# Batch 1's second pair summed on the vector engine, the tail put in another order, and empty slots that carry row numbers

## The reference

```python
xn = layernorm(x)                                   # x: [8, 512, 128]
# s: attention of each token over its own 16 heads (no sum over tokens)
q = xn @ Wq + bq                                    # [8, 512, 16, 8]
k, v = split((xn @ Wdown + bdown) @ Wup + bup)      # the same shape each
att = softmax(einsum('bthd,btgd->bthg', rope(q), rope(k)) / sqrt(8))
s = einsum('bthg,btgd->bthd', att, v) @ Wout + bout
# g: a transformer block on xn; its sequence is the batch axis (8, causal),
# then a mixture of 8 experts, 2 for each token, at most 1280 rows each
h1 = xn + proj(causal_attention(ln1(xn)))
z = ln2(h1)
p, i = top_k(softmax(z @ router), 2)                # p divided by its sum
h = h1 + sum over a token's 2 experts of p * gelu(z @ w1[i]) @ w2[i]
return x + s * silu(h)
```

## Time and profile before

| | us |
|---|---|
| median of 3 executions | 464.91 |
| lowest, highest | 464.27, 466.33 |
| the profiled execution | 464.99 |
| its span | 463.2 |
| mean granted PE clock (share of full speed) | 0.849 |

### The profile page before, as it was taken

The page is one execution under the profiler, slowest core; times in us unless marked ns, Lnnn a source line. Parts: engine busy times, 40 slices in busy tenths (PEclk is TensorE's granted clock), DMA queues, the critical chain, the costliest instruction groups (busy, mean ns, idle before and its releaser), DMA issues.

```text
span 463.2 us, 4715 instructions
## 1 busy us (share of the span) xinstructions
PE 337.6 (73%) x1518; PEld 247.7 (53%) x1518; DVE 382.1 (82%) x505; ACT 172.8 (37%) x382; POOL 254.4 (55%) x282
## 2 busy tenths in 40 slices
PE   1678986847834758864839997966999569739992
PEld 1565664635723623762626975745777356514852
DVE  5999599967979993799974986999997999780694
ACT  3475365262437100100104308626548544502311
POOL 0579446400005776877737757566977667537502
PEclk9955899786977659895869998988999797979997
DMA  8899910000000111011149112311234111149301
GB/s 206 151 193 200 316 49 2 0 0 2 0 0 29 53 52 52 2 52 52 52 124 257 51 35 59 114 60 53 80 110 121 57 40 47 40 140 297 91 0 45
DMA packets 53558, 38.06 MB, mean 82 GB/s; under 512 B 5337, under 2 KB 50206, under 8 KB 53534
## 3 DMA queue, kind: packets, MB, share of 16 engines
q1 hardware_dynamic: 48926, 28.25, 24.9%
q0 software_dynamic: 4608, 9.51, 6.1%
HBM read 16.55 MB, written 21.20 MB: 82 GB/s over the span
## 4 chain that ended last, share of the span: by engine, by line
PE 35%; DVE 18%; issue 17%; ACT 7%; another core or an unknown queue 3%; DMA 1%; SPq 0%; DVEq 0%; ACTq 0%
PE banks L944 10%; PE banks L916 5%; PE banks L923 4%; PE banks L931 4%; DVE prod L276 4%; PE banks L969 3%; DVE score L615 3%; PE banks L777 2%; ACT flat L1226 2%; DVE prod L285 1%; ACT flat L1240 1%; PE banks L955 1%; PE banks L957 1%; DVE stat L377 1%
## 5 line engine op out<-in xcount | busy, mean ns | idle before, releaser
L1326 POOL DMA_INDIRECT slot_rows<-rows_all,scatter_at x64 | 62.2, 972 | 75.9 <-DVE scatter_at L590 56.9
L1358 POOL DMA_INDIRECT expert_rows<-flat,to_at x80 | 79.1, 989 | 33.0 <-issue 21.5
L944 PE MATMUL banks<-prod,c_identf 128*128 128x256 f32 x256 | 62.8, 405 | 9.5 <-issue 9.2
L1301 POOL TENSOR_TENSOR prod<-rows_all,block_kv 128x64 f32<-128x64 f32 (+3 forms) x64 | 48.7, 796 | 36.9 <-ACT block_kv L1086 36.8
L944 PEld LDWEIGHTS banks<-prod,c_identf 128*128 128x128 f32 x256 | 52.4, 206 | 20.3 <-issue 12.1
L916 PE MATMUL banks<-flat 128*128 128x512 f32 (+1 forms) x96 | 41.0, 576 | 8.3 <-ACT flat L1226 6.4
L276 DVE TENSOR_TENSOR prod<-banks,qkv_h 128x2048 f32<-128x2048 f32 x20 | 44.8, 2282 | 0.6 <-DVE score L615 0.5
L615 DVE TENSOR_REDUCE score<-prod 128x512 f32<-128x4096 f32 x10 | 44.2, 4420 | 0.3
L285 DVE TENSOR_TENSOR prod<-score,banks 128x2048 f32<-128x2048 f32 x16 | 35.6, 2281 | 10.7 <-PE banks L931 10.5
L802 PE MATMUL banks<-wx,qkv_h 128*128 128x128 f32 x192 | 32.0, 328 | 11.9 <-ACT qkv_h L1105 6.7
L276 POOL TENSOR_TENSOR qkv_h<-block_kv,qkv_h 128x2048 f32<-128x2048 f32 x8 | 35.9, 4507 | 6.8 <-ACT block_kv L1110 6.7
(11 more groups left out here) (190 smaller groups left out, 586.0 us busy)
## 6 DMA issues: line engine op xcount, KB each, us to landing
slot_rows<-prod SPq DMA_DIRECT2D x10, 528.0 KB, 12.6
flat<-slot_rows SPq DMA_DIRECT2D x16, 264.0 KB
expert_rows<-prod SPq DMA_DIRECT2D x8, 512.0 KB, 6.9
flat<-expert_rows SPq DMA_DIRECT2D x8, 512.0 KB, 7.4
xn_all<-in_x SPq DMA_DIRECT2D x4, 512.0 KB, 4.9
flat<-in_w SPq DMA_DIRECT2D x16, 128.0 KB
out<-rows_all SPq DMA_DIRECT2D x7, 256.0 KB, 2.3
expert_rows<-flat,to_at POOLq DMA_INDIRECT x80
```

Source lines behind the costliest of these rows:

```text
L944: i = M.matmul(head_bank(s)[:, 2 * p * D:2 * (p + 1) * D].rearrange("p (a h d) -> p a h d", a=2, h=H), C["identf"][:], value_pair(s, p).re ...
L1301: Q.tensor_tensor(from_key(0, par, t).rearrange("p l (m d) -> p l m d", d=HD), q[:, :, t * QH:], block_key(h, par, t).unsqueeze(2).broadca ...
L1326: Q.indirect_dma_start(slots_d, bass.IndirectOffsetOnAxis(ap=scatter_at[:, k, n:n + 1], axis=0), z2x[:, h, s, part], None, element_offset= ...
L1358: Q.indirect_dma_start(expert_d, bass.IndirectOffsetOnAxis(ap=to_at[:, e % 2, a:a + 1], axis=0), ye[:, e % 2, a, :], None).then_inc(ye_out ...
```

## The change

**Empty slots.** The fill of the slots is no longer zeros. POOL clears a block of 128 x 2 x 10 x 132 floats (`empty`) at its start, waits for the constants and writes numbers of rows of `expert_rows` that nobody reads into column 1 (`TENSOR_SCALAR`, 20 elements for each partition). SP fills from it with 20 DMAs instead of 10, in a layout with 128 rows of each expert together. `expert_rows` is three rows longer. A slot of a second choice keeps the filled number in column 1, so DVE takes it off the number that it writes at the other end: two small steps more before `diff_done`, one more behind the slots' reduce, one less at the numbers.

**read_slots** keeps three of six operations (the steps that put numbers in the place of zeros are gone). Gates and numbers have three buffers instead of two, so that it waits for the work of e - 3, where it waited for e - 1 and e - 2; the scatters of e now wait for those of e - 2 themselves. The experts run in the order 0, 4, 1, 5, 2, 6, 3, 7 (`ORDER`).

The diff, cut to its core (`...` marks what is left out):

```diff
-PE_SCORES, SCORE_BANK = 1, (0, 7)
-
+PE_SCORES, SCORE_BANK = 1, 0
...
+
+AMID_SLOTS = {11: 0, 22: 1}
...
+ORDER = [i // 2 + i % 2 * (E // 2) for i in range(E)]
...
-EXPONENTIAL_AFTER = {0: 3, 2: 4, 7: 6}
+
+FIRST_EMPTY = 3
+
+EXPONENTIAL_AFTER = {0: 3, 2: 4}
...
-TAIL_BANKS = 4
-LAST_TURNED, LAST_OUT = (6, 0), (1, 2)
+TAIL_BANKS, PE_ROWS = 4, 6
+
+LAST_TURNED, LAST_OUT = (6, 0), (2, 3)
...
-    expert_d = nc.dram_tensor("expert_rows", (SLOTS + TOPK * CAP, D), F32, kind="Internal").ap()
+    expert_d = nc.dram_tensor("expert_rows", (SLOTS + TOPK * CAP + FIRST_EMPTY, D), F32, kind="Internal").ap()
...
-            sp.wait_ge(W["zero_done"], 1)
-            for k in range(CT):
-                sp.dma_start(slots_d[k * E * P:(k + 1) * E * P, :].rearrange("(p a) d -> p a d", p=P),
-                             zeros.broadcast_to([P, E, ROW])).then_inc(W["zero_out"], 16)
+            sp.wait_ge(W["empty_made"], 1)
+            for par in range(2):
+                for a in range(CT):
+                    sp.dma_start(slots_d[0:SLOTS, :].rearrange("(r e a p) d -> p r a e d", r=2, a=CT, p=P)[:, par, a],
+                                 empty[:, par, a:a + 1, :].broadcast_to([P, E // 2, ROW])).then_inc(W["zero_out"], 16)
...
                 sp.dma_start(expert_d[1 + s * E * P:1 + (s + 1) * E * P, :].rearrange("(p a) d -> p a d", p=P),
-                             zeros[:, :, 0:D].broadcast_to([P, E, D])).then_inc(W["zero_rows"], 16)
+                             empty[:, 0, 0:1, 2:2 + D].broadcast_to([P, E, D])).then_inc(W["zero_rows"], 16)
...
             def load_weights(e):
-                sp.dma_start(w1_sb[:, e % 2], w1[e]).then_inc(w_in[e % 2], 16)
-                sp.dma_start(w2_sb[:, e % 2], w2[e].rearrange("(f p) d -> p f d", p=P)).then_inc(w_in[e % 2], 16)
+                sp.dma_start(w1_sb[:, e % 2], w1[ORDER[e]]).then_inc(w_in[e % 2], 16)
+                sp.dma_start(w2_sb[:, e % 2], w2[ORDER[e]].rearrange("(f p) d -> p f d", p=P)).then_inc(w_in[e % 2], 16)
...
                 for q, (at, n) in enumerate(chunks):
-                    sp.dma_start(xe[:, e % 2, at // P:(at + n) // P], slots_d[e * CAP + at:e * CAP + at + n, :]
+                    sp.dma_start(xe[:, e % 2, at // P:(at + n) // P], slots_d[ORDER[e] * CAP + at:ORDER[e] * CAP + at + n, :]
...
+            less = mrow("dev2", 0, TT).rearrange("p (a s) -> p a s", s=S)
+            of_end = tmp1[:].rearrange("p (a s) -> p a s", s=S)
+            step(V.scalar_tensor_tensor(less, of_end, 2.0 * CAP, token_row(dump[:, 1], 0, TT), ALU.mult, ALU.subtract))
+            step(V.scalar_tensor_tensor(less, of_end, float(E // 2), less, ALU.is_le, ALU.add))
...
             told = [z2x[:, :, :, c].rearrange("p a s -> p a s") for c in (1, ROW - 1)]
-            for k in range(TOPK):
-                i = V.tensor_scalar(told[k], token_row(dump[:, k], 0, TT), float(1 - SLOTS), None, ALU.add)
+            V.tensor_scalar(told[0], token_row(dump[:, 0], 0, TT), float(1 - SLOTS), None, ALU.add)
...
             step(V.tensor_reduce(slot[:], placed, AX_X, ALU.add))
+            V.scalar_tensor_tensor(told[1], token_row(slot[:, 1], 0, TT), -2.0, less, ALU.mult, ALU.subtract)
...
                 wait_past(dve, "own", count["own"])
-                if s > PE_SCORES:
-                    dve.wait_ge(W["qk_summed"], 2)
...
                     m = qk_product(V, score_pair(s, p)[:, i, :], s, 2 * p + i)
-                if s == PE_SCORES:
+                if (s, p) == (PE_SCORES, 0):
...
+            def row_sum(s):
+
+                dve.wait_ge(moe_in[s], 16)
+                n = 2 * (s - PE_ROWS)
+                V.tensor_tensor(yg[:, s, :, 0, :], yg[:, s, :, 0, :], yg[:, s, :, 1, :], ALU.add).then_inc(W["row_sum"], 1)
+                dve.wait_ge(W["row_sum"], n + 1)
+                V.tensor_tensor(yg[:, s, :, 0, :], yg[:, s, :, 0, :], xn_all[:, :, s, :], ALU.add).then_inc(W["row_sum"], 1)
...
-            dve.wait_ge(W["zero_out"], 16 * CT)
+            dve.wait_ge(W["zero_out"], 16 * 2 * CT)
...
             for s in range(S):
-                differences(s)
+                if s < S - 1:
+                    differences(s)
...
                     normalize(s - 1)
+                if s == S - 2:
+                    differences(s + 1)
...
                 if s == S - 1:
-                    normalize(s - 1)
                     normalize_last(0)
+                    row_sum(s - 1)
...
                 if s == S - 1:
+                    normalize(s - 1)
                     normalize_last(1)
+                    row_sum(s)
...
             def attention_out(s):
-                pe.wait_ge(W["ao_done"], s + 1)
+
+                pe.wait_ge(W["ao_done"], s + 1 if s < S - 2 else S)
...
                 tail_start(s)
+            sum_values(6, 0)
...
                 tail_sum(s)
-            for s in range(TAIL_BANKS, 6):
+            sum_values(6, 1)
+            for s in range(TAIL_BANKS, PE_ROWS):
...
                 tail_sum(s)
-            sum_values(6, 0)
-            sum_values(6, 1)
-            for s in range(6, S):
-                tail_start(s)
-                tail_sum(s)
-
-            pe.wait_ge(W["silu_done"], 7)
+
+            pe.wait_ge(W["silu_done"], 5)
...
             def gates(s):
-                act.wait_ge(W["tail_sum"], s + 1)
                 act.wait_ge(W["v_ready"], s + 1)
-                A.activation(v_all[:, s, :], bank[s % TAIL_BANKS], ACT.Silu).then_inc(W["silu_done"], 1)
+                if s < PE_ROWS:
+                    act.wait_ge(W["tail_sum"], s + 1)
+                    A.activation(v_all[:, s, :], bank[s % TAIL_BANKS], ACT.Silu).then_inc(W["silu_done"], 1)
+                else:
+                    act.wait_ge(W["row_sum"], 2 * (s - PE_ROWS) + 2)
+                    A.activation(v_all[:, s, :].rearrange("p (a d) -> p a d", a=TT), yg[:, s, :, 0, :], ACT.Silu).then_inc(W["silu_done"], 1)
...
                     exponentials(EXPONENTIAL_AFTER[e])
+            exponentials(6)
+            exponentials(7)
             keep_attention(5)
-            for s in range(6):
-                gates(s)
-            exponentials(7)
-            for s in range(6, S):
+            for s in range(S - 1):
...
             keep_attention(6)
-            for p in range(2):
-                keep_attention_last(p)
+            keep_attention_last(0)
+            gates(S - 1)
+            keep_attention_last(1)
...
+
+            Q.memset(empty, 0.0).then_inc(W["empty_clear"], 1)
+            pool.wait_ge(W["consts_in"], n_consts)
+            pool.wait_ge(W["empty_clear"], 1)
+            Q.tensor_scalar(empty[:, :, :, 1], C["dump"][:].rearrange("p (k n) -> p k n", k=TOPK)[:, :, 0:CT], float(FIRST_EMPTY), None, ALU.add).then_inc(W["empty_made"], 1)
...
-            def score_products(s):
+            def score_products(s, tiles=(0, 1)):
...
                 wait_past(pool, "pool_read", n)
-                for i in range(2):
+                for i in tiles:
                     m = qk_product(Q, pool_prod[:, i], s, 2 + i, q_copy[:, s, i * D:(i + 1) * D])
-                m.then_inc(W["pool_made"], 1)
-
-            pool.wait_ge(W["zero_out"], 16 * CT)
+                if 1 in tiles:
+                    m.then_inc(W["pool_made"], 1)
+
+            pool.wait_ge(W["zero_out"], 16 * 2 * CT)
...
             for h in range(TT):
-                if h == TT // 2:
-                    for s in [i for i, after in POOL_SCORES.items() if after < 0]:
-                        score_products(s)
...
                 for s in range(S):
+                    if h * S + s in AMID_SLOTS:
+                        score_products(min(POOL_SCORES), (AMID_SLOTS[h * S + s],))
...
-                par = e % 2
+                par, at = e % 2, e % 3
...
                     pool.wait_ge(xe_in[3 * par + q], 16 * (e // 2 + 1))
-                wait_past(pool, "part_kept", PARTS * (e - 1))
-                wait_past(pool, ye_out[par], 16 * CT * (e // 2))
-                Q.tensor_tensor(gate_e[:, par], xe[:, par, :, 0], xe[:, par, :, ROW - 2], ALU.add).then_inc(W["gate_known"], 1)
-                Q.tensor_tensor(to_e[:, par], xe[:, par, :, 1], xe[:, par, :, ROW - 1], ALU.add).then_inc(W["told"], 1)
+                if e >= 3:
+                    pool.wait_ge(W["part_kept"], PARTS * (e - 2))
+                    pool.wait_ge(ye_out[(e - 3) % 2], 16 * CT * ((e - 3) // 2 + 1))
+                Q.tensor_tensor(gate_e[:, at], xe[:, par, :, 0], xe[:, par, :, ROW - 2], ALU.add).then_inc(W["gate_known"], 1)
+                Q.tensor_tensor(to_e[:, at], xe[:, par, :, 1], xe[:, par, :, ROW - 1], ALU.add).then_inc(W["told"], 1)
                 pool.wait_ge(W["told"], e + 1)
-                Q.tensor_scalar(none_e[:, par], to_e[:, par], 0.0, None, ALU.is_equal).then_inc(W["to_known"], 1)
-                pool.wait_ge(W["to_known"], 4 * e + 1)
-                Q.tensor_tensor(none_e[:, par], none_e[:, par], C["dump"][:, par * NT:par * NT + CT], ALU.mult).then_inc(W["to_known"], 1)
```

(10 more changed lines are left out.)

46 lines of the change are left out of this document (21 added, 25 removed).

## The result

The changed kernel takes 448.06 us (median of 4, 446.96 to 449.58), the kernel before 465.62 on the same chip; the ratio is 0.9634, with a 95% interval of 0.9588 to 0.9681. The forecast was 443.0 with 438 to 453. The profiled execution has a span of 445.1 us, 18.1 less than before, where 22.0 less were forecast.

The account below looks back on a forecast made before the run. DVE was taken as the bound, its attention chain meeting POOL's scatters at the end. Terms summed to -23.8 us, so 441.2, plus 1.8 for unseen costs: 443.0; own range 438 to 448, 80% range 438 to 453.

Parts of the forecast that it names:

- the tail: End of kernel: batch 7's exponential before all silus, -17.85 us; row_sum(6) +1.5, late attention_out(6) +3.8.
- first rival: Batch 1: PE stays held in the value sums, expert rows land 6.3 us late, time 447.5; chance 0.22.
- What bounds the kernel: Whole kernel: DVE, busy 382.1 of 463.2 us; largest wait 17.85, batch 7's exponential behind six silus on ACT.
- values(0, 1): DVE in batch 1: wait of 10.54 us goes, as PE sums half the scores and POOL pauses after 22 scatters.
- The open term, the second wait: DVE before normalize(1): wait of 8.87 us for PE's value sums stays, change 0, bounds -1.7 to +5.4.
- The experts: Experts 4 to 7: POOL's shorter gap between bursts brings each to 15.2 us, -1.0 each, -4.0 together.
- second rival: Experts don't get quicker and nothing else moves them, first load stays at 411.42, time 451; chance 0.15.
- slower rival: Gap of 1.1 us between POOL's bursts too short, PE's results wait, up to 6.6 us per expert, 476; chance 0.03.
- Additions beside POOL: DVE's additions while POOL works: cost taken in with other unseen costs, 1.8 us together, bounds 0 to 3.5.
- the 1.8: Allowance without a place for held PE completions, routing's steps and additions beside POOL: 1.8 us, bounds 0 to 3.5.
- From normalize(6) to the end: Tail: 7.92 us from PE's L952 to DVE's end now follow normalize(6), a net cost of +3.8 us.
- The clock: PE before normalize(1): a rule on idle gaps would lose up to 6.9 us; no loss taken, tail loss covered.

Follow-up runs that it names:

- a_tail: The changed kernel with the old tail (exponential of batch 7 behind six silus, normalize(6) between the halves): ratio 0.986 to the kernel before.
- a_mid32: The changed kernel with POOL's two products of batch 3 back behind 32 scatters: end 310.1 us behind the first scatter (changed kernel 308.8), no ratio.
- a_batch1: The changed kernel with PE summing the scores of both pairs of batch 1 again: end 310.0 us behind the first scatter (changed kernel 308.8), no ratio.
- a_half: The changed kernel with only the first five of each expert's ten scatters, so incomplete output: end 304.0 us behind the first scatter (changed kernel 308.8).
- a_pause: The changed kernel with POOL also waiting before tile 7's scatter, for experts 1, 3 to 6, for PE's next-expert group: ratio 0.955 to the kernel before.
- a_best: The changed kernel with about 1 us of POOL work within each burst, batch 7's exponential later and attention_out(6) before the bias: ratio 0.941 to the kernel before.
- a_warm: The kernel with those three edits, but bias products ahead of attention_out(6) again and each issued three times: ratio 0.948 to the kernel before.

## Why the prediction was right, and where its steps were not

The direction, the main cause (the tail) and the range were right; the size was 5 us too good, just outside the narrower range of its own sum (to 448). By the first traces the error is larger: 18.1 - 6.62 = 11.5 us came behind the first scatter where 22.0 were forecast, and an early first scatter filled a part of the rest. How much of that is luck depends on the trace of before: 11.5, 14.9 or 18.6. The number nearest to the measured 448.06 is the first rival's 447.5, and that is chance: what it was worked out from did not happen.

- **What bounds the kernel**: right. The tail's wait was the largest, it went whole, and nothing took its place; a_tail puts the new tail at about 10 where the terms gave 12.5.
- **values(0, 1)**: the size and the release were right, and one of the two causes wrong. POOL's first pause came at 167.84 - 3.49 = 164.35, 28.0 behind the first scatter as worked out, and PE ended the first pair's sums in it, at 170.48; DVE came for them at about 175.6 and didn't wait. a_mid32 brings the wait back. That PE does half of the sums has no part in it, as a_batch1 shows. The reading behind it was off: the row of 15.79 us has 29 of the 32 matmuls, and DVE waited for the first 16 only, so the delay was some 12 us and not 5. For the 4.42 us that DVE now spends on the second pair's reduce, it got 1.85 + 3.45 + 0.85 us of shorter waits (before differences(1), normalize(0) and normalize(1)), by a_batch1 against the changed kernel.
- **The open term, the second wait**, was taken as unchanged with a bound of -1.7. It came out at -2.6, and for another reason than the one worked out. PE ended batch 1's value sums at 226.26, but DVE went on at 233.06, 2.5 behind POOL's last scatter: it waited for a result that was ready. Expert 0 began 98.7 behind the first scatter, 7.2 earlier than before (6.3 forecast), and now waits 8.72 us for its slots, not for PE's sums. So the first rival, PE held in batch 1's sums as before, falls.
- **The experts**: the step that failed. Forecast were 4.0 us over experts 4 to 7, on the ground that POOL's gap falls to 1.1 and PE and ACT allow 15.2. The gap became a wait for ACT (3.82 us where 3.55 stood). The 15.2 rested on 14.55, which is the distance from the second group of gates of expert 5 to the first of expert 6, while the first group of expert 5 had started at 358.18; it isn't what PE and ACT need, which is 13.3 by a_half. What held the experts in both kernels is that PE's results reach ACT late during POOL's long bursts. From the start of expert 1 to SP's first load it was 278.94 to 411.42 before, 132.5 us, and is 269.82 to 401.85, 132.0. The second rival (the experts don't get quicker) describes this part; the slower rival's mechanism is real, as a_pause shows, but POOL's running dry gave the gap back, as was argued against it.
- **Between experts 0 and 1** a loss stood nowhere in the sum. It took 30.1 us before and 34.8 after. POOL's first burst now ends with `read_slots` at 262.45, just when PE has turned batch 1's heads (261.58 + 0.60), and ACT gets them 1.9 later, at 264.11; before, POOL's burst had ended 2 us ahead of them. PE then runs L979 and L981 at the lower clock. The late copy (1.9) and the lower clock (2.2, in L979, L981, L825 and L932) make up most of the 4.7. With it the exponential of batch 3 and the whole chain of experts move, and DVE waits 2.91 more here and 3.11 more at batch 5, where 2.0 less were forecast. Most of the earlier expert 0 was lost in this place.
- **Additions beside POOL**: costs of this kind were put into the 1.8, without a place. They were 3.39 (L643) and 1.9 (row_sum(6), 3.36 instead of 1.5). L643 takes 1.23 alone and 4.62 where POOL's products ran from 240.09 to 249.08; L687 takes 1.75 beside POOL's gates, and the same addition 0.68 where POOL does nothing (in a_best at 422.87). The Trainium skill ("SBUF — State Buffer", section "Who interferes with whom") says that a tensor_tensor of DVE with both inputs in SBUF contends with GpSimd's reads, and that the shared port is an exclusive lock for which the order of issue decides who blocks; the trace agrees, L643 ended 1.1 us after POOL's product and L687 0.55 us after POOL's gate.
- **From normalize(6) to the end**: mis-sized, 10.36 us where 7.92 was forecast. PE still had the sums of batches 4 and 5 and the bias to do and began 1.6 late, at 431.37; from there it took 8.74.
- **The clock**: no loss was taken. In front of normalize(1), PE's value sums of batches 0 and 1 took 16.21 and 15.91 us instead of 13.81, at granted clocks of 0.85 and 0.88, the first behind 5.13 us of idle time; these 2 us each cost nothing, since PE then waited for the slots. In the tail the value sums of batch 6 ran at full clock behind no idle time. In a_warm PE idled 9.29 us before the first half, which then took 10.2 instead of 7.1, as the rule of the Trainium skill cited in the prediction would have it; the fall at 425 in the same trace had no idle time before it.

## What to carry to other kernels

Where two chains meet, a gain on one turns into a wait on it until the other is shortened too: write down for every gain who is late next, and check it by undoing the parts one by one and reading positions, not only times. A gap on an engine that is busy nearly all the time may be what lets others get on; before it is filled, ask what is released in it, and try to put a short stop where it is missing. And a difference in a stretch that the change doesn't touch should be looked for in a second trace of the old kernel before it is explained.

## What the runs showed of the hardware

While POOL issues indirect DMAs one after the other, what PE has finished can reach ACT and DVE late, and PE's own next matmuls then come in ones and twos ("issue" gaps of 0.3 to 3.1 us). These results came 1.7 to 4.9 us after POOL stopped: ACT's copy for batch 3 (22.87 us of idle time before it in the kernel before, 10.29 in the changed one, 2.9 and 3.0 behind the last scatter; 4.7 in a_mid32), DVE's values(0, 1) in a_mid32 (4.9), ACT's gates of expert 5 (1.9), its copy behind expert 0 (1.7), and a_pause (1.9, 17 scatters nearly in a row). With bursts of five scatters ACT's gates no longer wait for it, and with a stop of 1 to 2 us in the middle of ten it is less.

A long row of scatters doesn't always hold, and a stop isn't the only release. In the changed kernel ACT took four of PE's results without delay (its copies L1125 at 143.29 to 151.55, 7 to 15 us behind the first scatter). In the kernel before, PE's L957 ended at 219.86, 24 us into a row of scatters that ended at 236.6, and ACT copied its result at 225.08, 5.2 late but without any stop of POOL:

```profile
225.08 0.59 ACT L1248 COPY qkv_h<-banks 128x512 f32<-128x512 f32 x1 [9.35 <-remote]
```

So when the hold sets in is open, and so is by which path POOL's scatters and PE's signals touch.

PE's granted clock in the first 50 us differs from one execution to the next (0.50 to 1.00 from 38 to 50 us), and the first scatter with it by up to 6.9 us; in the kernel before most of that is lost again before expert 0.
